# Expert tiles from two lists, the last sequence's routing among the tiles, ten sequences' sums beside the last 39 tiles

## The chip, the core and the metric

The kernel runs on one core of a Trainium2 chip. Times are device microseconds (us) of one execution. The engines are TensorE (PE; its weight loads are PEld), VectorE (DVE), ScalarE (ACT), GpSimd (POOL) and SyncE (SP); SP, ACT and POOL also issue transfers (DMA). Each engine works through its own instructions in order, and waits for the others on semaphores.

## What is computed

16 sequences of 512 tokens with 128 features pass a state-space mixer, then a layer of 8 experts of which each token takes the best 2. Cut to what matters here:

```python
x = layernorm(x + mixer(x))                     # sequence by sequence: conv, scan in chunks of 128, gate
gates = sigmoid(u @ centroids.T)                # 8192 tokens x 8 experts
topk_vals, topk_idx = top_k(gates, 2)           # two experts for each token
h = gelu(einsum('nd,edf->enf', u, W1) + b1)     # 128 -> 512
outs = einsum('enf,efd->end', h, W2) + b2       # 512 -> 128
x = layernorm(x + sum over the two of gate * out)
```

## The kernel before

It has three stages, one after the other.

**Mixer.** A slot for each sequence s (`slots`, `slot_pe`, `slot_dve` and so on). Beside the scan of sequence s, a slot projects sequence s+1 and routes sequence s-1: normalisation, logits, gates, the two picks, ranks within each expert by matmuls against a mask. The rows of sequence s-2 are written by indirect transfers from POOL (`scatter`, eight for each sequence) into `sorted_rows` in DRAM, which holds a region for each expert. `next_row` counts the rows of each expert. A last slot, 16, routes sequence 15 alone.

**Experts.** When all rows are placed, DVE makes a table of 136 tiles of 128 rows (first row and expert of each), and unused rows are filled with padding (`write_pads`). Then, for tile j: SP loads the 128 rows (`xs`, ring of 8); PE transposes them (L631), multiplies by the expert's W1 (`up`, L637) and, after ACT's gelu (L856), by W2 (`down`, L649); DVE copies the transposed rows (L1205), the expert's W1 (L1209) and b2 (L1210) into place, and after `down` adds the bias (L1218) and scales and adds (L1221); POOL writes the result to `moe_rows` by an indirect transfer (L1450). PE's order in an iteration is transpose(j+2), up(j+1), down(j); DVE's is fetch(j+2), weigh(j). Each of them reads the expert number from the table into a register first (`value_load`). The tiles run in loops that the hardware repeats (`Fori`), but for the first 8 and the last 16, which are written out.

**Last stage.** For each sequence n: SP loads two blocks of 256 KB of `moe_rows`, DVE and POOL add them (L1250, L1464), DVE takes mean and variance (L1265, L1273, L1278), POOL the root (L1470), DVE the bias (L1256), ACT normalises (L877) and issues the store. A partition p holds the tokens p, p+128, p+256 and p+384 of a sequence.

## Time and profile before

| | |
|---|---|
| median of 3 runs | 807.89 us (805.18 to 808.49) |
| profiled execution | 798.2 us, span of its instructions 796.3 us |
| busy over the span | PE 673.3, PEld 548.5, DVE 600.1, ACT 473.8, POOL 465.2 us |
| mixer until PE's last mixer matmul | to about 425 us |
| first to last expert tile (start of `down`) | 467.62 to 740.20 us |
| last stage | from there to 796.3 us |

The span runs from the first to the last instruction. Busy time of PE counts pipelined matmuls, so that a full PE shows 99% and not its peak. An engine's idle time is printed in brackets ahead of an instruction, with what ended it. A line number of the profile is that of the kernel before.

### The profile page before, as it was taken

How to read it: one execution, taken by the hardware profiler on the slowest of the kernel's cores; microseconds unless marked ns; L12 is line 12 of the kernel's file. 1: busy time of each engine (PE TensorE's matmuls, PEld its weight loads, DVE VectorE, ACT ScalarE, POOL GpSimd, SP SyncE). 2: the span in 40 equal slices, each digit the busy share in tenths (PEclk: the TensorE clock that was granted, in tenths of full speed). 3: DMA queues.
4: the chain of work that ended last, by engine and by line, in shares of the span. 5: the costliest groups of instructions: out<-in, count | busy, mean ns of one | idle time of the engine just before them, and what ended most of it. 6: DMA issues, size and time to landing. Idle time of an engine off the chain costs nothing.

```text
span 796.3 us, 21108 instructions
## 1 busy us (share of the span) xinstructions
PE 673.3 (85%) x5092; PEld 548.5 (69%) x5093; DVE 600.1 (75%) x2000; ACT 473.8 (60%) x1179; POOL 465.2 (58%) x642
## 2 busy tenths in 40 slices
PE   7969999999999999999984079999999999999200
PEld 6846666666666566666663069999999999999100
DVE  4388989998999999899974446677766667677485
ACT  3747777677677677677661045555555555555165
POOL 4023377777777777777777715555555555555464
PEclk9999999999999999999997579999999999999755
DMA  9160010111110111110100212222222222222496
GB/s 260 32 240 14 16 41 18 41 32 34 42 41 19 38 31 39 42 33 26 38 18 31 73 46 69 64 62 65 65 66 66 61 63 66 66 66 61 132 302 200
DMA packets 74802, 54.09 MB, mean 68 GB/s; under 512 B 9436, under 2 KB 70111, under 8 KB 74481
## 3 DMA queue, kind: packets, MB, share of 16 engines
q1 hardware_dynamic: 56400, 31.90, 15.3%
q0 software_dynamic: 8448, 16.93, 6.4%
q10 hardware_dynamic: 9888, 4.49, 2.0%
q8 instruction: 29, 0.48, 0.3%
q14 instruction: 37, 0.30, 0.1%
HBM read 31.11 MB, written 22.69 MB: 68 GB/s over the span
## 4 chain that ended last, share of the span: by engine, by line
PE 69%; DVE 9%; issue 8%; POOL 5%; ACT 4%; DMA 3%; DVEq 1%; SPq 0%; ACTq 0%; POOLq 0%
PE pl L637 16%; PE p L649 15%; PE pj L402 4%; PE p L589 4%; PE p L597 3%; POOL sorted_rows L1382 3%; PE p L551 2%; PE pj L631 2%; PE p L545 2%; ACT pair L816 2%; PE pj L410 2%; PE p L499 2%; PE p L527 2%; PE p L410 2%; PE pl L446 2%
## 5 line engine op out<-in xcount | busy, mean ns | idle before, releaser
L1450 POOL DMA_INDIRECT moe_rows<-yv,xs x136 | 147.3, 1083 | 139.4 <-DVE yv L1221 122.0
L856 ACT ACTIVATE L<-pl,b_sb 128x128 f32<-128x128 f32 x544 | 154.9, 368 | 118.8 <-PE pl L637 118.8
L637 PE MATMUL pl<-Btok,M 128*128 128x128 f32 x1088 | 151.8, 283 | 0.9 <-DVE M L1209 0.3
L1382 POOL DMA_INDIRECT sorted_rows<-pair,slot x128 | 128.3, 1002 | 35.2 <-issue 33.6
L929 DVE SCALAR_TENSOR_TENSOR acc<-pj,conv_w_sb,acc 128x511 f32<-128x511 f32 (+2 forms) x192 | 142.5, 742 | 4.0 <-ACT acc L734 1.1
L649 PE MATMUL p<-w,L 128*128 x1088 | 143.9, 275 | 1.6 <-ACT L L856 1.6
L637 PEld LDWEIGHTS pl<-Btok,M 128*128 128x128 f32 x1088 | 133.4, 193 | 5.1 <-DVE M L1209 2.7
L649 PEld LDWEIGHTS p<-w,L 128*128 128x128 f32 x1088 | 132.4, 192 | 2.0 <-issue 2.0
L1205 DVE COPY Btok<-pj 128x128 f32<-128x128 f32 x136 | 39.7, 292 | 76.5 <-PE pl L637 66.8
L734 ACT ACTIVATE acc<-pj,conv_b_sb,conv_w_sb 128x512 f32<-128x512 f32 x64 | 49.5, 773 | 33.1 <-PE pj L402 33.1
L402 PE MATMUL pj<-xT,w_xbc 128*128 128x512 f32 x128 | 66.7, 603 | 0.0
L545 PEld LDWEIGHTS p<-M,Xdt 128*64 128x64 f32 x512 | 27.6, 137 | 51.6 <-issue 49.8
L1395 POOL TENSOR_TENSOR Xdd<-Xdt,cur 128x256 f32<-128x256 f32 x48 | 29.5, 615 | 55.9 <-DVE Xdt L1080 47.4
L631 PE MATMUL pj<-ident,xs 128*128 128x128 f32 x136 | 40.1, 295 | 25.8 <-DMA xs<-sorted_rows 24.0
L1209 DVE COPY M<-w 128x512 f32 x136 | 57.4, 422 | 0.4 <-issue 0.4
L1345 POOL TENSOR_TENSOR gt<-yv,sz 128x256 f32<-128x256 f32 x64 | 47.1, 736 | 11.3 <-DVE yv L1106 10.6
L1221 DVE SCALAR_TENSOR_TENSOR yv<-yv,xs 128x128 f32<-128x128 f32 x136 | 47.8, 352 | 4.8
L1218 DVE TENSOR_TENSOR yv<-p,b2e_mem 128x128 f32<-128x128 f32 x136 | 39.6, 291 | 13.7 <-PE p L649 7.5
L545 PE MATMUL p<-M,Xdt 128*64 128x128 f32 x512 | 42.5, 286 | 8.7 <-issue 5.9
L692 ACT ACTIVATE pl<-pl 128x512 f32<-128x512 f32 x64 | 37.5, 586 | 15.7 <-PE pl L428 15.5
L1003 DVE TENSOR_TENSOR M<-pl,Gm 128x512 f32<-128x512 f32 x64 | 43.9, 686 | 2.0 <-ACT pl L692 1.4
L1080 DVE TENSOR_TENSOR Xdt<-p,cur 128x256 f32<-128x256 f32 x64 | 27.0, 422 | 20.5 <-ACT Btok L802 10.4
(203 smaller groups left out, 1328.4 us busy)
## 6 DMA issues: line engine op xcount, KB each, us to landing
xs<-sorted_rows SPq DMA_DIRECT2D x136, 65.0 KB, 1.8
xres<-in_x SPq DMA_DIRECT2D x16, 256.0 KB, 3.0
w<-in_w SPq DMA_DIRECT2D x2, 2048.0 KB, 10.3
acc<-moe_rows SPq DMA_DIRECT2D x16, 256.0 KB, 4.1
xc<-moe_rows SPq DMA_DIRECT2D x16, 256.0 KB, 5.1
out<-sz ACTq DMA_DIRECT2D x16, 256.0 KB, 5.1
moe_rows<-yv,xs POOLq DMA_INDIRECT x136, 2.4
sorted_rows<-pair,slot POOLq DMA_INDIRECT x128, 2.4
```

Source lines behind the costliest of these rows:

```text
L402: pe.matmul(pj[k % 2][:, :], w_xbc[:, k * P:(k + 1) * P], xT[:, q.n, :], start=True, stop=True).then_inc(proj_psum, 1)
L545: mm = pe.matmul(p7[half, (h // 2) * P:(h // 2 + 1) * P], Xdt[c % 2][:, h * HD:(h + 1) * HD], M[c % 2][:, h, :], start=(h < 2), stop=(c == ...
L631: pe.transpose(pj[k % 2][:, 0:P], xs[k][:, 0:P], ident[:, :]).then_inc(sT_psum, 1)
L637: mm = pe.matmul(pl[k % 2][:, f * P:(f + 1) * P], w1e[k % 2][:, f * P:(f + 1) * P], sT[k % 2][:, :], start=True, stop=True)
L649: mm = pe.matmul(o[:, 0:P], hT[k % 2][:, f, :], w2[:, bass.ds(e, 1), f, :].rearrange("p e d -> p (e d)"), start=(f == 0), stop=(f == FB - 1))
L734: act.activation(acc[:, c, :], pj[c % 2][:, :], ACT.Identity, bias=conv_b[:, c:c + 1], scale=conv_w[:, c, TAPS - 1:TAPS]).then_inc(tap0_do ...
L856: act.activation(hT[k % 2][:, f, :], pl[k % 2][:, f * P:(f + 1) * P], ACT.Gelu, bias=b1[:, bass.ds(e * FB + f, 1)]).then_inc(hT_ready, 1)
L929: ins = dve.scalar_tensor_tensor(out=acc[:, k, j:TOKS], in0=pj[k % 2][:, 0:TOKS - j], scalar=conv_w[:, k, TAPS - 1 - j:TAPS - j], in1=acc[ ...
L1209: dve.tensor_copy(w1e[k % 2], w1[:, bass.ds(e, 1), :].rearrange("p e f -> p (e f)")).then_inc(w1e_ready, 1)
L1221: dve.scalar_tensor_tensor(out=ye[k % 4], in0=ye[k % 4], scalar=xs[k][:, P + 1:P + 2], in1=xs[k][:, 0:P], op0=ALU.mult, op1=ALU.add).then_ ...
L1382: pool.indirect_dma_start(out=sorted_rows[:, :], out_offset=bass.IndirectOffsetOnAxis(slot[q.par][:, c, k:k + 1], 0), in_=(rowA, rowB)[k][ ...
L1450: pool.indirect_dma_start(out=moe_rows[:, :], out_offset=bass.IndirectOffsetOnAxis(xs[k][:, P:P + 1].bitcast(I32), 0), in_=ye[k % 4], in_o ...
```

## The change

- **Two lists of tiles.** The first 72 tiles (`FULL`) are whole tiles of the rows of the first 10 sequences (`EARLY`). Their table is worked out on DVE in slot 15 in two parts (`early_table`), with the tile number along the partitions, and goes to DRAM and back by two small transfers to lie in one partition (`table_away`, `table_back`). The other 63 tiles have a second list, made among tiles 4 to 40.
- **Routing among the tiles.** Slot 16 is gone. Tiles start after slot 15, and the routing of sequence 15 and the last steps of 14 are set between tiles 0 to 53 on all engines; POOL's last 16 scatters stand at every third tile. The 8 pad writes all stand on SP ahead of the load of tile 46.
- **Sums beside tiles.** From tile 94 on, one of the first ten sequences' final steps stands in every 4 tiles: DVE's addition at the first, statistics at the second, moments and variance at the third, POOL's root at the fourth, ACT's output 8 tiles later. SP loads its two blocks after the row load of tile 97+4n. Six sequences are left for the last stage.
- **Four consecutive tokens per partition** in the last stage, so that a partition's piece of a block is 2 KB and no longer four pieces of 512 B.
- 135 tiles and not 136, all written out with no hardware loop; the tile buffers lie in `xT` and no longer in the scan's buffers.

```diff
-TILES = 2 * TOKENS // P + E
+TILES = 2 * TOKENS // P + E - 1
+EARLY = 10
+FULL = 72
+COVER = 88
+LATE = TILES - FULL
+SEGS = 2 * E
+FIN_TILES = 4
+FIN_AT = COVER + 6
...
-        sT = Btok
-        w1e = [M[i][:, :, :].rearrange("p h s -> p (h s)") for i in range(2)]
-        hT = L
+        w1e = [xT[:, i, :] for i in range(2)]
+        hT = [xT[:, 2 + i, :].rearrange("p (f s) -> p f s", f=FB) for i in range(2)]
+        sT = [xT[:, 4, i * P:(i + 1) * P] for i in range(2)]
         b2e = [b2e_mem[:, i, :] for i in range(4)]
-        ye = [yv[i // 2][:, i % 2, :] for i in range(4)]
+        ye = [xT[:, 5, i * P:(i + 1) * P] for i in range(4)]
...
-        out_seq = out.rearrange("b (c p) d -> b p c d", p=P)
-        moe_seq = moe_rows.rearrange("(k b c p) d -> b p k c d", k=2, b=SEQS, p=P)
+        out_seq = out.rearrange("b (p c) d -> b p c d", p=P)
+        moe_seq = moe_rows.rearrange("(k b p c) d -> b p k c d", k=2, b=SEQS, p=P)
...
-            for k in range(-1, SEQS + 1):
+            for k in range(-1, SEQS):
...
+            def table_away(k, lo, hi):
+                dq.wait_ge(found_ready, k + 1)
+                dq.dma_start(tile_list[lo:hi, :], found[k][0:hi - lo, :]).then_inc(table_out, 16)
+            def table_back(k, lo, hi):
+                dq.wait_ge(table_out, 16 * (k + 1))
+                dq.dma_start(table[0:1, 2 * lo:2 * hi],
+                             tile_list[lo:hi, :].rearrange("j k -> (j k)").unsqueeze(0)).then_inc(table_in, 16)
+            def load_rows(j):
+                k = j % RING
+                table_known(dq, j)
+                wait(dq, rows_out[k], 16 * (j // RING))
+                at = dq.value_load(table[0:1, 2 * j:2 * j + 1], min_val=0, max_val=SPARE + (E - 2) * P)
                 dq.dma_start(xs[k][:, :], sorted_rows[bass.ds(at, P), :]).then_inc(xs_in[k], 16)
-            for k in range(RING):
-                load_rows(k, k, 0)
-            with dq.Fori(1, TILES // RING) as i:
-                for k in range(RING):
-                    load_rows(RING * i + k, k, i)
-            for k in range(RING):
-                dq.wait_ge(rows_out[k], 16 * TILES // RING)
-            def load_moe(turn, i):
-                n = FIN * turn + i
+            def load_moe(n):
+                i = n % FIN
                 wait(dq, moe_sum, n - FIN + 1)
                 wait(dq, fve_ready, n - FIN + 1)
                 for k in range(2):
                     dq.dma_start(yy[i][:, k], moe_seq[n, :, k]).then_inc(yy_in[i], 16)
-            for i in range(FIN):
-                load_moe(0, i)
-            with dq.Fori(1, SEQS // FIN) as turn:
-                for i in range(FIN):
-                    load_moe(turn, i)
+            table_away(0, 0, FULL)
+            table_back(0, 0, FULL)
+            for i in range(2):
+                for k in range(2):
+                    dq.wait_ge(scattered[i][k], 16 * NC * EARLY // 2)
+            for j in range(TILES):
+                if j == 46:
+                    write_pads(dq, range(E))
+                if j == 56:
+                    table_away(1, FULL, TILES)
+                if j == 60:
+                    table_back(1, FULL, TILES)
+                if j == FULL:
+                    dq.wait_ge(pads_in, 16 * E)
+                    dq.wait_ge(spare_in, 16 * E)
+                    for i in range(2):
+                        for k in range(2):
+                            dq.wait_ge(scattered[i][k], 16 * NC * SEQS // 2)
+                load_rows(j)
+                if j == COVER + RING:
+                    for k in range(RING):
+                        dq.wait_ge(rows_out[k], 16 * COVER // RING)
+                if j > COVER + RING and (j - COVER - RING - 1) % FIN_TILES == 0:
+                    load_moe((j - COVER - RING - 1) // FIN_TILES)
+            for k in range(RING):
+                dq.wait_ge(rows_out[k], 16 * ((TILES - 1 - k) // RING + 1))
+            for n in range(EARLY, SEQS):
...
+            def transpose_rows(j):
+                pe.wait_ge(xs_in[j % RING], 16 * (j // RING + 1))
+                wait(pe, fetched, j - 1)
+                pe.transpose(pj[j % 2][:, 0:P], xs[j % RING][:, 0:P], ident[:, :]).then_inc(sT_psum, 1)
+            def up(j):
+                pe.wait_ge(w1e_ready, j + 1)
+                wait(pe, hT_ready, FB * (j - 1))
+                for f in range(FB):
+                    mm = pe.matmul(pl[j % 2][:, f * P:(f + 1) * P], w1e[j % 2][:, f * P:(f + 1) * P],
+                                   sT[j % 2], start=True, stop=True)
+                mm.then_inc(h_psum, 1)
...
+                if not project:
+                    transpose_rows(0)
+                    transpose_rows(1)
...
+                if not project:
+                    up(0)
...
+            for j in range(TILES):
+                if j == 10:
+                    turn_rows(last)
+                if j == 14:
+                    logits(last)
+                if j == 24:
+                    ranks(last)
+                if j + 2 < TILES:
+                    transpose_rows(j + 2)
+                if j + 1 < TILES:
+                    up(j + 1)
+                down(j)
...
+            for j in range(TILES):
+                if 4 <= j < 4 + NC:
+                    normalise(last, j - 4)
+                if j == 12:
+                    keep_turned(last)
+                if j == 13:
+                    second_rows(last)
+                if j == 16:
+                    exp_logits(last)
+                n, step = divmod(j - FIN_AT - 8, FIN_TILES)
+                if 0 <= n < sent and step < 2:
+                    finish(n, step)
+                if 0 <= n < sent and step == 2:
+                    send(n)
+                gelu(j)
...
+            def early_table(part):
+                full = starts[:, 0, :]
+                if part == 0:
+                    count_tiles(starts[:, 0:2, :])
+                    in_table(dve.tensor_copy(q_tiles[:, 0:E], full))
+                    tiles_ahead(E, E)
+                    return
+                in_table(dve.scalar_tensor_tensor(out=jump[:, 1:E + 1], in0=ends[:, 0:E], scalar=-float(P),
+                                                  in1=seg_row[:, 0:E], op0=ALU.mult, op1=ALU.add))
+                row_steps(E)
+                find_tiles(0, E)
...
+            def fetch(j):
+                e = expert_of(dve, j)
+                wait(dve, h_psum, j - 1)
+                dve.wait_ge(sT_psum, j + 1)
+                dve.tensor_copy(sT[j % 2], pj[j % 2][:, 0:P]).then_inc(fetched, 1)
+                dve.tensor_copy(w1e[j % 2], w1[:, bass.ds(e, 1), :].rearrange("p e f -> p (e f)")).then_inc(w1e_ready, 1)
+                dve.tensor_copy(b2e[j % 4], b2[:, bass.ds(e, 1), :].rearrange("p e d -> p (e d)")).then_inc(b2e_ready, 1)
...
+            for j in range(TILES):
+                if j == 0:
+                    statistics(last)
+                if j == 1:
+                    take_ranks(Seq(0, SEQS - 2))
+                if j == 2:
+                    shift_rows(last)
+                if j == 4:
+                    late_starts()
+                if j == 18:
+                    gate_values(last)
+                if j == 19:
+                    gate_tops(last)
+                if j == 20:
+                    gate_places(last)
+                if j == 21:
+                    gate_picks(last)
+                if j == 26:
+                    take_ranks(last)
+                if j == 27:
+                    dve.wait_ge(rank_read, SEQS)
+                    dve.tensor_copy(pad_at[:, :], next_row[:, :]).then_inc(pads_known, 1)
+                if j == 30:
+                    late_counts()
+                if j == 33:
+                    tiles_ahead(SEGS + 1, SEGS)
+                if j == 36:
+                    late_jumps()
+                if j == 38:
+                    row_steps(SEGS + 1)
+                if j == 40:
+                    find_tiles(1, SEGS + 1)
+                n, step = divmod(j - FIN_AT, FIN_TILES)
+                if 0 <= n < EARLY and step == 0:
+                    add_rows(n)
+                if 0 <= n < EARLY and step == 1:
+                    out_statistics(n)
+                    if n > 0:
+                        minus_mean(n - 1)
+                if 0 <= n < EARLY and step == 2:
+                    out_moments(n)
+                    out_variance(n)
+                if j + 2 < TILES:
+                    fetch(j + 2)
+                weigh(j)
...
+            root_rows(Seq(0, SEQS - 1))
+            place_rows(Seq(0, SEQS - 2))
+            for j in range(TILES):
+                for r, first in ((Seq(0, SEQS - 2), 2), (Seq(0, SEQS - 1), 32)):
+                    at, step = divmod(j - first, 3)
+                    if 0 <= at < 2 * NC and step == 0:
+                        scatter(r, at % NC, at // NC)
+                if j == 29:
+                    place_rows(Seq(0, SEQS - 1))
+                n, step = divmod(j - FIN_AT, FIN_TILES)
+                if 0 <= n < EARLY and step == 0:
+                    add_experts(n)
+                if 0 <= n < EARLY and step == 3:
+                    root(n)
+                store(j)
```

`fetch` and `weigh` are DVE's steps of a tile as before, with one more semaphore; `late_starts`, `late_counts`, `late_jumps`, `row_steps`, `tiles_ahead` and `find_tiles` are chains of small DVE operations on 8 to 272 elements, each of which waits for the one before it.

How the order moves, at three places. DVE, one tile before (one of the last 16), from the bias addition on; `TENSOR_LOAD` is the read of the expert number:

```order
L1218 TENSOR_TENSOR yv<-p,b2e_mem 128x128 [waits rows_out0,b2e_ready,ye_psum]
L1221 SCALAR_TENSOR_TENSOR yv<-yv,xs 128x128 [waits biased]
L1200 TENSOR_LOAD table
L1200 ISA x2
L1205 COPY Btok<-pj 128x128 [waits sT_psum,h_psum]
L1209 ISA
L1209 COPY M<-w 128x512
L1210 ISA
L1210 COPY b2e_mem<-b_sb 128x128
```

DVE after, from the bias addition of tile 95 into tile 96, where `BN_AGGR` and L1375 are the moments and the variance of sequence 0 in the last stage:

```order
L1235 TENSOR_TENSOR xT<-p,b2e_mem 128x128 [waits rows_out3,b2e_ready,ye_psum]
L1238 SCALAR_TENSOR_TENSOR xT<-xT,xs 128x128 [waits biased]
L1368 BN_AGGR fmv<-fst 128x2 [waits fin_step,const_ready]
L1368 BN_AGGR fmv<-fst 128x2 x3
L1375 TENSOR_SCALAR fve<-fmv 128x4 [waits fin_step]
L351 TENSOR_LOAD table [waits table_in]
L351 ISA x2
L1225 COPY xT<-pj 128x128 [waits sT_psum,h_psum]
L1226 ISA
L1226 COPY xT<-w 128x512
L1227 ISA
```

The last-stage work stands between the scaling of a tile and the read for the next fetch, so the copies of the next W1 come behind it.

PE at the end of slot 15 before, with `ones,ysq` and `w_out,gt` the last mixer products, `chosen` the ranks and `ident,pair` the first step in routing sequence 15:

```order
L589 MATMUL p<-ones,ysq 128x96 x8
L597 MATMUL p<-w_out,gt 128x128 x8
L613 MATMUL p<-chosen,ones_b 128x32
L614 MATMUL p<-chosen,before_b 128x32
L617 MATMUL p<-chosen,ones_b 128x24
L617 MATMUL p<-chosen,ones_b 128x16
L617 MATMUL p<-chosen,ones_b 128x8
L570 MATMUL p<-ident,pair 128x128 x4
L575 MATMUL p<-w_gate,uT 128x96 x4
L613 MATMUL p<-chosen,ones_b 128x32
```

PE after, at the same place, with L585 the transposes of tile rows and L591 `up`:

```order
L653 MATMUL p<-ident,carried 128x128 x2
L585 MATMUL pj<-ident,xs 128x128 x2
L686 MATMUL p<-ones,ysq 128x96 x8
L694 MATMUL p<-w_out,gt 128x128 x8
L591 MATMUL pl<-xT 128x128 x4
L574 MATMUL p<-chosen,ones_b 128x32
L575 MATMUL p<-chosen,before_b 128x32
L578 MATMUL p<-chosen,ones_b 128x24
L578 MATMUL p<-chosen,ones_b 128x16
L578 MATMUL p<-chosen,ones_b 128x8
L585 MATMUL pj<-ident,xs 128x128
L591 MATMUL pl<-xT 128x128 x4
```

The transposes of tiles 0 and 1 now stand ahead of the last mixer products, `up` of tile 0 ahead of the ranks of 14, and nothing of sequence 15's routing is left there.

SP before, where the loads of rows enter the loop:

```order
L368 DMA xs<-sorted_rows 128x130
L372 UNCONDITIONAL_BRANCH
L372 ISA
L367 ISA
L367 TENSOR_LOAD table
L367 ISA x2
L368 ISA
L368 DMA xs<-sorted_rows 128x130
```

SP after, from the load of the rows of tile 45 on:

```order
L405 TENSOR_LOAD table
L405 ISA x2
L406 ISA
L406 DMA xs<-sorted_rows 128x130
L357 TENSOR_LOAD pad_at
L357 ISA x2
L358 ISA
L358 DMA sorted_rows<-pad_tile 128x130
```

Such a read of `pad_at` and the pad write behind it come eight times on SP before the rows of tile 46 are loaded.

## Rows read from the trace of the kernel before

**Rows 1.** Windows: stretch, length, PE, PEld, DVE, ACT, POOL busy, granted clock, DMA share, GB/s.

```profile
420.00:430.00 10.00, 4.18 (x37) 3.92 (x37) 5.84 (x37) 0.98 (x3) 8.72 (x12) 0.92 0.11 35
430.00:440.00 10.00, 3.43 (x17) 2.71 (x17) 2.86 (x21) 2.38 (x6) 6.04 (x11) 0.50 0.08 27
500.00:600.00 100.00, 98.64 (x835) 95.38 (x835) 68.75 (x245) 55.86 (x196) 54.83 (x49) 1.00 0.25 64
```

**Rows 2.** Timeline from slot 15 to the first tile: start, duration, instruction, idle before.

```profile
414.70 0.42 DVE L1080 TENSOR_TENSOR Xdt<-p,cur 128x256 f32<-128x256 f32 x1 [2.36 <-ACT Btok L802]
...
423.26 2.05 PE L597 MATMUL p<-w_out,gt 128*128 128x128 f32 x16 [0.37 <-POOL gt L1345]
...
446.27 0.17 DVE L1171 TENSOR_SCALAR tb<-tb 128x8 f32<-128x8 f32 x1
446.48 0.17 DVE L1172 CAST tbi<-tb 128x8 int32<-128x8 f32 x1
...
447.15 4.12 SPq L323 DMA_DIRECT2D sorted_rows<-pad_tile  x4
...
459.64 8.09 SPq L368 DMA_DIRECT2D xs<-sorted_rows  x8
...
461.54 0.45 PE L631 MATMUL pj<-ident,xs 128*128 128x128 f32 x1 [23.24 <-DMA xs<-sorted_rows]
...
465.05 1.28 ACT L856 ACT_TABLE_LOAD   x1 [29.82 <-PE pl L637]
```

**Rows 3.** Timeline: one looped tile's copy, then one written-out tile.

```profile
525.41 0.29 DVE L1205 COPY Btok<-pj 128x128 f32<-128x128 f32 x1 [0.48 <-PE pl L637]
...
718.67 0.35 DVE L1221 SCALAR_TENSOR_TENSOR yv<-yv,xs 128x128 f32<-128x128 f32 x1
...
719.38 0.29 DVE L1205 COPY Btok<-pj 128x128 f32<-128x128 f32 x1 [0.36 <-PE pl L637]
719.46 1.14 ACT L856 ACTIVATE L<-pl,b_sb 128x128 f32<-128x128 f32 x4 [0.77 <-PE pl L637]
719.59 0.42 DVE L1209 COPY M<-w 128x512 f32 x1
...
720.06 0.97 PEld L637 LDWEIGHTS pl<-Btok,M 128*128 128x128 f32 x8
...
720.26 0.29 DVE L1218 TENSOR_TENSOR yv<-p,b2e_mem 128x128 f32<-128x128 f32 x1
```

**Rows 4.** Timeline of PE: `down` of tiles 0, 8, 120, 134 and 135.

```profile
467.62 1.15 PE L649 MATMUL p<-w,L 128*128 x8 [1.10 <-ACT L L856]
...
483.68 1.06 PE L649 MATMUL p<-w,L 128*128 x8
...
711.49 0.72 PE L649 MATMUL p<-w,L 128*128 x5
...
738.62 1.06 PE L649 MATMUL p<-w,L 128*128 x8
740.20 1.15 PE L649 MATMUL p<-w,L 128*128 x8 [0.52 <-ACT L L856]
```

**Rows 5.** Timeline of the last stage: first sequences, and the last addition.

```profile
748.94 0.56 DVE L1250 TENSOR_TENSOR xc<-acc 128x384 f32<-128x384 f32 x1 [6.87 <-DMA acc<-moe_rows]
...
749.91 0.87 DVE L1265 BATCH_NORM_STATS2 fst<-xc 128x6 f32<-128x128 f32 x4 [0.41 <-POOL xc L1464]
750.89 0.38 DVE L1273 BATCH_NORM_AGGREGATE fmv<-fst 128x2 f32<-128x6 f32 x4
...
751.94 0.82 POOL L1464 TENSOR_TENSOR xc<-acc 128x128 f32<-128x128 f32 x1 [2.13 <-DMA acc<-moe_rows]
752.37 0.42 DVE L1278 TENSOR_SCALAR fve<-fmv 128x4 f32<-128x4 f32 x1
...
752.87 1.04 POOL L1470 TENSOR_TENSOR frs<-fve,neg_half 128x4 f32<-128x4 f32 x1
...
786.36 0.52 DVE L1250 TENSOR_TENSOR xc<-xc 128x384 f32<-128x384 f32 x1
```

539 lines of the change are left out of this document (269 added, 270 removed).

## Prediction

> **What bounds the kernel now.** I read the windows by stage first, then the timeline at the two changes of stage, then single tiles. In the expert stage PE is busy 98.64 of 100 us and DVE 68.75 [rows 1], so PE looks like the only limit. The timeline of one tile says more [rows 3]. After the scaling L1221 (start 718.67, 0.35 us) DVE sits idle for 0.36 us and then copies rows and W1; the W1 copy ends at 719.59 + 0.42 = 720.01, and PE's next `up` loads weights at 720.06. The bias addition of the next tile follows at 720.26. So DVE goes round in the same time as PE and has no slack: what stands between L1221 and L1209 delays `up`. The 0.36 us is the read of the expert number: 0.71 us from the start of L1221 to the copy, half of it behind L1221. In a looped tile the idle is 0.48 us [rows 3], for there DVE also has to compute addresses. That shows in the pace: tiles 8 to 120 take 711.49 - 483.68 = 227.81 us, 2.034 us each; the written-out tiles 120 to 134 take 27.13 us, 1.938 us each [rows 4].
>
> Between the stages PE stands still. Its last mixer product of weight starts at 423.26 (2.05 us); the first rows are asked for at 459.64, transposed at 461.54, and `down` of tile 0 starts at 467.62 [rows 2, 4]. From 740.20, the last `down` [rows 4], to the end at 796.3 are 56.1 us in which PE has nothing. There the 16 additions L1250 start from 748.94 to 786.36 [rows 5], 37.42 us over 15 intervals, 2.495 us each.
>
> **The change, part by part.** All times are in the profiled execution (span 796.3, execution 798.2 us).
>
> *Start of the tiles.* The first list costs DVE 7 small chained steps in chunk 0 of slot 15 and 9 in chunk 1. Such steps of 8 elements follow each other at 446.48 - 446.27 = 0.21 us [rows 2]: 1.5 and 1.9 us. The first part has no cover that I see and moves the slot by 1.5 us. The second fits into DVE's idle 2.36 us ahead of 414.70 [rows 2] and ends near 416.1. Two small transfers follow; the nearest row is a row load, 461.54 - 459.64 = 1.9 us [rows 2], so 3.8 us; then a read (0.7) and the load (1.9): rows of tile 0 at 422.5, of tile 1 1.0 us later (8 loads take 8.09 us on SP [rows 2]). PE's transposes of both stand ahead of products that would start about 422.4 now, so PE waits until near 423.9; L597 moves from 423.26 to about 426.3, `up` of tile 0 ends near 429.3. ACT loads its gelu table (1.28 us [rows 2]) and takes 1.14 us [rows 3]: `down` 0 at 432.0. DVE meanwhile does the statistics of sequence 15 (0.87 + 0.38 and gaps [rows 5]) before it fetches tile 2; its W1 is there at 432.5, and with `up` and `down` of 0.97 us each behind it `down` 1 starts at 434.2. Bounds: 430 if the transfers hide wholly, 439 if each takes 2 us more.
>
> *Pace.* All tiles are written out, and DVE's rows of a tile are the same instructions as in the last 16 before, so 133 more tiles at 1.938 us: 257.8 us. At the looped pace it would be 12.8 us more; that is the upper bound.
>
> *Routing and second list among tiles 1 to 53.* An addition of x between L1221 and the read costs x less what the 0.36 us hides; where the read itself waits for the last step, it costs x + 0.35. DVE: 21 chained steps at 0.21 (two of 272 elements at 0.4) and five such reads, 6.6 us; ranks of 14 and 15 and the four pieces of the gates, 3.8 us: 10.4. PE: 4 transposes, 4 logit and 5 rank matmuls, about a tile's worth, 2.1. ACT: the exponential at tile 16 changes the table and back, 2 x 1.28 + 0.2, less its 0.77 idle [rows 3] and the 0.5 before `down` needs it: 1.5; its other pieces of 0.4 to 0.6 us fit the idle. SP: 8 pad writes at 4.12/4 = 1.03 us [rows 2] hold the load of tile 46 for 8.2 us. That load can go when tile 38 is stored, about 7.3 us before PE wants it, and lands in 1.9: 5.5 us are covered, 2.7 stall. POOL's scatters and `place_rows` fit: 54.83 us busy of 100 [rows 1]. Sum 16.7 us; bounds 8 (half of DVE hidden) and 22.
>
> *Sums beside the last tiles.* For each sequence DVE gets an addition 0.56, statistics 0.87 with a bias 0.16, moments 0.38 with a variance 0.16 [rows 5], the two 0.16 as small steps go [rows 2]. By the rule above: 0.35 + 0.56 + 0.03 - 0.71 = 0.23; 0.35 + 1.03 + 0.03 - 0.71 = 0.70; the variance waits for the moments, so 0.41 + 0.05 + 0.35 = 0.81. That is 1.74, and I take 1.9 since POOL and DVE disturb each other (next part): 19 us for ten. Bounds: all 2.13 us less three times 0.36, 1.05 us; and all 2.13 plus a read and gaps, 2.6 us. ACT's halves of 0.83 us fit its 0.77 idle and the 0.5 behind; POOL has half a tile free. Each transfer has about 4.4 us from its issue to DVE's addition.
>
> *POOL beside DVE.* The variance L1278 takes 0.42 us at 752.37 while POOL's addition runs from 751.94 for 0.82 us [rows 5]; a step of that kind takes 0.17 alone [rows 2]. So they do hold each other up by some 0.25 us a time, and the 1.9 above has 0.16 for it. The Trainium skill (SBUF — State Buffer, SBUF: two separate sides) says that the port pair that both share is an exclusive lock for a whole instruction, taken by GpSimd and by VectorE's two-port copies. This trace shows the 0.42 us, no copy beside a root. By that rule ten sums would cost up to POOL's 1.86 us each more, 18.6 us, and not 1.6.
>
> *End.* Ten intervals less in the last stage: 10 x 2.495 = 25.0 us. Two waits for transfers go too, with 2 KB pieces, 0.6 us: bounds 0 and 3. Left: 56.1 - 25.6 = 30.5 us.
>
> **Sum.** 434.2 + 257.8 + 16.7 + 19.0 = 727.7 for the last `down`, plus 30.5: a span of 758.2 against 796.3, 38.1 us less. The execution of 798.2 us would be 760.1. The median of the runs, 807.89, lies 9.7 us above the profiled one; I take the same 38.1 us off it: 769.8, said as **770 us**.
>
> **Rivals.**
> - *More of DVE's work hides* than I count: 1.05 us a sum (-8.5) and half of 10.4 (-5): 756 us. For it: the read may run beside several queued steps. Against: `up` starts right on the heels of the copy [rows 3].
> - *POOL's instructions lock out DVE's copies.* POOL's root of 1.04 and addition of 0.82 us [rows 5] would each stop DVE if it comes to L1209, L1210 or L1221, about half of its time: 10 x 0.93 = 9 us more, 779 us. For it: the 0.42 us. Against: a root is 4 elements and may hold nothing for most of its time. The skill's rule above is this one.
> - *The blocks come late.* DVE waits in order at L1250, ahead of the next fetch. If a pair of blocks takes 6.5 us and not some 4, ten waits of 2 us: 790 us. Against: tile traffic is 64 GB/s [rows 1], and only one pair is under way.
> - *PE's clock falls, slower than before.* It was granted 0.92 with PE busy 4.18 of 10 us, and 0.50 at 3.43 of 10 [rows 1]. If the gaps of up to 0.8 us beside the last 39 tiles lowered it to 1.2 GHz, PE would need 1.94 us more a tile; 20 tiles use up the 38.1 us, all 39 would give 770 + 76 = 846 us. Against: PE stays about 80% busy there, twice what kept 0.92.
> - *Nothing gained*: the written-out code stalls on its own fetches by 0.28 us a tile. The 14 written-out tiles at 1.938 us speak against it.
>
> **Chances.** Forecast 0.55 (760 to 780), more hides 0.15, lock 0.16, late blocks 0.07, slower clock 0.04, nothing 0.03. The range that holds 8 in 10 takes in the second and third and part of the fourth: 755 to 786. A measurement of this kernel can tell about 0.5% from no change. Faster by over 0.5%: 0.93; within it: 0.03; slower: 0.04.
>
> **What would show it.** `down` of tile 1 near 434 with the granted clock 1.00 through 420 to 440; tiles without additions at 1.94 us; a stall of PE near tile 46 with SP's pads ahead of it; groups of four tiles from 94 on at 7.75 + 1.9 = 9.7 us, with the gap ahead of `up` ended by DVE's W1 copy; L1209's copies longer than 0.42 us if the lock is real; no idle of DVE on `moe_rows` blocks in the tiles; 30.5 us from the last `down` to the end. The prediction is wrong if DVE's additions cost nothing, or if the gap before tile 0 stays.

## The result, and the profile after

The changed kernel takes 798.08 us (median of 4 runs, 796.57 to 801.27) beside 806.94 us for the kernel before on the same chip: 0.992 of it, with an interval of 0.989 to 0.994. So it is faster, by 0.8% and not by the forecast 4.7%. The profiled execution took 799.25 us with a span of 797.4 us, 1.1 us more than that of before. The profiled execution of before, 798.2 us, is 8.7 us quicker than the median of its runs; that of after is 1.2 us slower than its own. So the spans below miss the forecast by 39 us, and the medians by 28 (798.08 beside 770).

Set beside the steps of the forecast, the span of 797.4 splits up like this:

| step | forecast | measured | difference |
|---|---|---|---|
| `down` of tile 1 | at 434.2 | at 442.13 | +7.9 |
| tiles 1 to 59 | 129.1 us | 600.55 - 442.13 = 158.4 us | **+29.3** |
| tiles 59 to 94 | 67.8 us | 668.84 - 600.55 = 68.3 us | +0.5 |
| tiles 94 to 134 | 96.5 us | 764.91 - 668.84 = 96.1 us | -0.4 |
| from the last `down` to the end | 30.5 us | 797.4 - 764.91 = 32.5 us | +2.0 |

(129.1 is 58 tiles at 1.938 and the 16.7 us of routing; 96.5 is 40 tiles and the 19 us of sums.) The windows of after, with the columns of [rows 1], show the same:

```profile
430.00:440.00 10.00, 8.31 (x55) 8.11 (x55) 5.74 (x37) 2.42 (x5) 4.61 (x5) 0.74 0.25 62
440.00:460.00 20.00, 14.98 (x115) 14.27 (x116) 10.49 (x43) 9.50 (x33) 10.67 (x18) 0.89 0.14 38
500.00:600.00 100.00, 81.07 (x645) 76.87 (x644) 57.14 (x212) 43.01 (x152) 48.54 (x57) 0.95 0.23 64
600.00:660.00 60.00, 58.92 (x524) 58.44 (x523) 43.05 (x155) 34.68 (x123) 30.22 (x32) 1.00 0.27 71
```

From 500 to 600 PE, full before with 98.64 of 100 us [rows 1], is busy 81.07, and no other engine is fuller than it was. From 600 on it is full again. So something stops the engines again and again in the first 58 tiles.

Beside the last 39 tiles the time in all is as forecast. PE's `down` of tiles 94 to 98:

```profile
668.84 1.06 PE L601 MATMUL p<-w,xT 128*128 x8
672.00 1.06 PE L601 MATMUL p<-w,xT 128*128 x8
674.29 1.06 PE L601 MATMUL p<-w,xT 128*128 x8
676.68 1.06 PE L601 MATMUL p<-w,xT 128*128 x8
678.57 1.06 PE L601 MATMUL p<-w,xT 128*128 x8
```

The four intervals of 3.16, 2.29, 2.39 and 1.89 make 9.73 us; the forecast said 9.7. (The sum agrees, the parts don't; see the section on why the prediction was wrong.)

Which wait is it in tiles 1 to 59? The list of waits from 440 to 760 us (engine, line, what ended the wait: us in all, times, longest) has two entries whose ender the profile can't name, and before has none of this kind:

```profile
DVE xT L1235 <- remote: 21.8, 11, 5.4
ACT xT L919 <- remote: 19.5, 6, 5.6
```

41.3 us together, in part at the same time. L1235 is the bias addition behind `down`, L919 the gelu behind `up`; both wait for PE. One of these places, in the timeline (lines of PEld and of others left out):

```profile
498.03 0.97 POOL L1613 DMA_INDIRECT moe_rows<-xT,xs  x1 [0.71 <-issue]
...
498.55 1.16 PE L591 MATMUL pl<-xT 128*128 128x128 f32 x8
...
499.30 0.96 POOL L1546 DMA_INDIRECT sorted_rows<-pair,slot  x1 [0.30 <-issue]
...
499.55 1.06 PE L601 MATMUL p<-w,xT 128*128 x8
...
500.57 0.98 POOL L1613 DMA_INDIRECT moe_rows<-xT,xs  x1 [0.30 <-issue]
...
502.42 1.14 ACT L919 ACTIVATE xT<-pl,b_sb 128x128 f32<-128x128 f32 x4 [3.46 <-remote]
502.47 0.29 DVE L1235 TENSOR_TENSOR xT<-p,b2e_mem 128x128 f32<-128x128 f32 x1 [0.87 <-remote]
```

`up` (L591) ends at 499.71 by the trace, and ACT's gelu starts 2.71 us later. `down` (L601) ends at 500.61, and DVE's addition starts 1.86 us later. ACT and DVE go on within 0.05 us of each other. Such places are found by what stands ahead of them: POOL issues a routing scatter (L1546) between two stores (L1613), each 1.27 us behind the last, and everything goes on 3.1 us after the scatter's start. 502.42 - 499.30 is 3.12; the places at 476.41, 510.84, 540.67 and 548.30 stand 3.1 to 3.2 us behind scatters at 473.3, 507.7, 537.5 and 545.2. The change sets 16 scatters among tiles 2 to 53, and 29.3 / 16 = 1.8 us. They make 13 such places. The first two, at 449.89 and 455.18, stand in a row of six transfers without a gap and share the longest: `gelu` starts at 455.92 behind an `up` that ended at 451.41. Those at 554.34 and 561.74 have the next store 2.3 and 4.4 us behind them and make none.

I call such a place a hold. Theory H: the holds are the missing time, and they come from the scatters. Rivals: P, POOL's time for a scatter makes the stores late; F, the written-out code waits for its own fetches; D, DVE's added work and cross waits.

### The profile page after: what moved, and what is told of

Its sections match the earlier page's. It is cut to its first block, busy times and chain, and to the rows that moved or that the text cites. A ratio compares the mean times of both kernels' runs of the same rounds, so it can differ in the third digit from the quotient of the medians.

```text
span 797.4 us, 20105 instructions
## 1 busy us (share of the span) xinstructions
PE 678.0 (85%) x5075; PEld 549.4 (69%) x5075; DVE 591.9 (74%) x2009; ACT 474.0 (59%) x1176; POOL 455.3 (57%) x648
## 4 chain that ended last, share of the span: by engine, by line
PE 60%; issue 12%; DVE 12%; ACT 4%; POOL 3%; DMA 3%; another core or an unknown queue 2%; SPq 2%; DVEq 2%; ACTq 0%; POOLq 0%
PE pl L591 9%; PE p L601 9%; PE pj L455 5%; PE p L686 4%; PE p L653 4%; PE p L694 3%; PE p L647 3%; PE p L629 3%; PE p L552 2%; PE p L566 2%; PE p L463 2%; PE p L662 2%; POOL moe_rows L1613 2%; PE pl L499 2%
## 5 line engine op out<-in xcount | busy, mean ns | idle before, releaser
L919 ACT ACTIVATE xT<-pl,b_sb 128x128 f32<-128x128 f32 x540 | 153.5, 368 | 153.6 <-PE pl L591 114.5
L1613 POOL DMA_INDIRECT moe_rows<-xT,xs x135 | 135.0, 1000 | 148.5 <-DVE xT L1238 92.5
L591 PE MATMUL pl<-xT 128*128 128x128 f32 x1080 | 151.6, 284 | 27.5 <-DVE xT L1226 24.0
L601 PE MATMUL p<-w,xT 128*128 x1080 | 148.3, 282 | 18.1 <-ACT xT L919 17.9
L591 PEld LDWEIGHTS pl<-xT 128*128 128x128 f32 x1080 | 134.1, 195 | 38.8 <-DVE xT L1226 31.7
L601 PEld LDWEIGHTS p<-w,xT 128*128 128x128 f32 x1080 | 135.4, 197 | 20.4 <-issue 20.1
L1546 POOL DMA_INDIRECT sorted_rows<-pair,slot x128 | 127.7, 998 | 32.6 <-issue 32.6
L1235 DVE TENSOR_TENSOR xT<-p,b2e_mem 128x128 f32<-128x128 f32 x135 | 39.0, 289 | 53.2 <-PE p L601 26.1
L1225 DVE COPY xT<-pj 128x128 f32<-128x128 f32 x135 | 39.3, 291 | 52.4 <-PE pl L591 23.5
L1226 DVE COPY xT<-w 128x512 f32 x135 | 57.2, 424 | 0.2 <-issue 0.2
L1238 DVE SCALAR_TENSOR_TENSOR xT<-xT,xs 128x128 f32<-128x128 f32 x135 | 48.4, 359 | 4.8
L585 PE MATMUL pj<-ident,xs 128*128 128x128 f32 x135 | 37.7, 279 | 6.4 <-DMA xs<-sorted_rows 6.4
```

Source lines behind the costliest of these rows:

```text
L591: mm = pe.matmul(pl[j % 2][:, f * P:(f + 1) * P], w1e[j % 2][:, f * P:(f + 1) * P], sT[j % 2], start=True, stop=True)
L601: mm = pe.matmul(o[:, 0:P], hT[j % 2][:, f, :], w2[:, bass.ds(e, 1), f, :].rearrange("p e d -> p (e d)"), start=(f == 0), stop=(f == FB - 1))
L919: act.activation(hT[j % 2][:, f, :], pl[j % 2][:, f * P:(f + 1) * P], ACT.Gelu, bias=b1[:, bass.ds(e * FB + f, 1)]).then_inc(hT_ready, 1)
L1226: dve.tensor_copy(w1e[j % 2], w1[:, bass.ds(e, 1), :].rearrange("p e f -> p (e f)")).then_inc(w1e_ready, 1)
L1238: dve.scalar_tensor_tensor(out=ye[j % 4], in0=ye[j % 4], scalar=xs[k][:, P + 1:P + 2], in1=xs[k][:, 0:P], op0=ALU.mult, op1=ALU.add).then_ ...
L1546: pool.indirect_dma_start(out=sorted_rows[:, :], out_offset=bass.IndirectOffsetOnAxis(slot[q.par][:, c, k:k + 1], 0), in_=(rowA, rowB)[k][ ...
```

## The experiments

Ratios are to the kernel before on the same chip, whose median was 803.34, 802.35, 797.12, 797.45, 796.26 and 802.04 us in the six sets. The changed kernel was not run again in these sets; its 0.992 is 796.7 us on the first chip and 790.5 on the third, each to within some 2 us.

**Scatters replaced by POOL's work.**

```diff
-                        scatter(r, at % NC, at // NC)
+                        pool.tensor_tensor(idle_out[:, 8 * (first == 32) + at, :], neg_half[:, :], neg_half[:, :], ALU.pow)
```

The rows of the last two sequences are then never placed; to keep the tiles whole, 32 more pad blocks are written at the start, and two sums read other rows.

> The changed kernel with its 16 scatters among the tiles (sequences 14 and 15) replaced by 16 POOL powers of 128x4 (about 1.04 us each, as the scatter's 0.97 us of POOL), so the rows of these two sequences are never placed and their sums read sequence 13; loads, stores and products keep their number. Theory H (a scatter between two stores holds back what PE signals, and everything goes on 3.1 us after the scatter's start): the stalls of tiles 5 to 57 go, tiles 1 to 59 take about 129 us instead of 158, the whole about 798 - 29 = 769 us. Rival P (it is POOL's time, which makes the stores late): no change, 798. Rival F (the written-out code waits for its own fetches) and rival D (VectorE's added work and cross waits): no change, 795 to 799.

Measured: 767.77 us, 0.958 (0.954 to 0.962), 28.9 us less than the changed kernel there. H holds; P, F and D fall as causes of these 29 us, for POOL has the same time, the code is as long, and DVE's work is all there. `down` of tiles 1 and 59:

```profile
438.96 1.06 PE L606 MATMUL p<-w,xT 128*128 x8
...
568.67 1.06 PE L606 MATMUL p<-w,xT 128*128 x8
```

That is 129.7 us beside the forecast 129.1, so the term for routing and second list was right in sum. Not all of the 29 us is time in holds. The windows of tiles 1 to 59, the changed kernel's first:

```profile
442.00:600.00 158.00, 126.01 (x1002) 119.69 (x1001) 87.73 (x338) 70.90 (x241) 77.39 (x92) 0.95 0.22 59
439.00:569.00 130.00, 116.89 (x1008) 112.72 (x1007) 86.98 (x338) 71.32 (x242) 80.02 (x92) 1.00 0.24 64
```

The granted clock is 0.95 beside 1.00, and PE is busy 9 us longer for about the same products. So up to 9 of the 29 us are products at the slower clock, behind the longer holds; they are counted in the 1.8 us a scatter.

**Each scatter twice**, the second into a tensor that nothing reads:

```diff
                         scatter(r, at % NC, at // NC)
+                        scatter_again(r, at % NC, at // NC)
```

> The changed kernel with each of the 16 scatters among the tiles issued twice, the second time into a tensor that nothing reads. H: each hold lasts one indirect transfer (1.27 us) longer, 16 x 1.3 = 21 us more, about 819 us; with the second not adding to the hold, 798. Rival P: at most 16 x 1.3 less what the 0.9 us gaps of POOL take back, 800 to 810. F and D: no change.

Measured: 814.58 us, 1.016 (1.012 to 1.020), 17.9 us more than the changed kernel, 1.1 us for each second scatter. H said 21.

**The same in the looped kernel before**, behind every fourth store, with 128 rows, with 16 rows, and as a transfer without offsets:

```diff
                     oob_is_err=False).then_inc(rows_out[k], 16)
+                if k % 4 == 3:
+                    pool.indirect_dma_start(
+                        out=rows_again[:, :],
+                        out_offset=bass.IndirectOffsetOnAxis(slot[1][:, k // 4, 0:1], 0),
+                        in_=rowA[1][:, k // 4, :], in_offset=None).then_inc(again, 16)
```

> The kernel before, tile loops still in hardware loops, with one more scatter of the last sequence's rows (into a tensor that nothing reads) behind every fourth store: 34 scatters between stores. H: 34 stalls of some 1.8 us, about 807 + 61 = 868 us. If the hold needs something of the changed kernel, or P: POOL has 34 x 1.3 = 44 us more in 136 gaps of 0.9 us = 122 us, so no change, 807 to 812. F, D: 807.

> The kernel before with an extra scatter behind every fourth store as in the last extra-scatter run, but of 16 rows instead of 128. If the hold goes with the work of the transfer (descriptors and packets): nearly none, 803 to 812 us. If it goes with the instruction (0.97 us of POOL and a second one close behind): the full 1.8 us each, about 864 us.

> The kernel before with, behind every fourth store, a direct transfer of the same 128 rows from POOL's queue (no offsets) in place of the extra scatter. If any transfer that POOL issues between two stores holds what PE signals: about 864 us. If it has to be an indirect one: 803 to 806 us.

Measured: 864.28 us, 1.076 (1.072 to 1.080) with 128 rows; 864.77 us, 1.076 (1.073 to 1.079) with 16; 801.95 us, 0.999 (0.998 to 1.001) without offsets. 60.9 us for 34 scatters are 1.79 us each. So the hold isn't a matter of the changed kernel's code, nor of rows and packets; it takes the indirect instruction. (The direct transfers stood as close, 0.96 to 1.20 us behind one store and 0.9 to 1.8 ahead of the next, and took 0.59 us of POOL each.) The Trainium skill (DMA: Bandwidth & Descriptors, SWDGE vs HWDGE vs iDMA) says that a core of GpSimd computes and writes the descriptors for direct and indirect transfers alike. That gives no reason why one should hold and the other not; the runs show that they differ. The hold in the looped kernel, with 128 rows:

```profile
548.16 1.20 POOL L1453 DMA_INDIRECT moe_rows<-yv,xs  x1 [0.99 <-issue]
...
549.56 1.06 PE L652 MATMUL p<-w,L 128*128 x8
549.66 0.97 POOL L1458 DMA_INDIRECT rows_again<-pair,slot  x1 [0.30 <-issue]
...
550.93 0.99 POOL L1453 DMA_INDIRECT moe_rows<-yv,xs  x1 [0.30 <-issue]
...
552.58 0.29 DVE L1221 TENSOR_TENSOR yv<-p,b2e_mem 128x128 f32<-128x128 f32 x1 [1.93 <-remote]
```

The extra transfer needn't be a scatter of rows, nor be there at all. In the run with direct transfers one place holds, and there three of the kernel's own stores follow one another, 1.3 us apart:

```profile
661.41 0.99 POOL L1453 DMA_INDIRECT moe_rows<-yv,xs  x1 [0.30 <-issue]
...
662.41 1.06 PE L652 MATMUL p<-w,L 128*128 x8
...
662.71 0.99 POOL L1453 DMA_INDIRECT moe_rows<-yv,xs  x1 [0.31 <-issue]
...
664.00 0.98 POOL L1453 DMA_INDIRECT moe_rows<-yv,xs  x1 [0.30 <-issue]
...
665.74 0.29 DVE L1221 TENSOR_TENSOR yv<-p,b2e_mem 128x128 f32<-128x128 f32 x1 [1.99 <-PE p L652]
```

`down` ends at 663.47 and the addition starts 2.27 us later, 3.03 us behind the store in the middle. The changed kernel has such a place too, far behind its scatters: stores at 653.74 and 655.02, `down` ended at 655.26, the addition at 656.61. So the scatters matter because they bring indirect transfers close together, where stores alone mostly stand 1.9 us apart. But not every close row holds: in the kernel before four stores from 702.70 to 706.57 hold nothing.

**The kernel before with its tile loops written out**, nothing else:

```diff
-            with pe.Fori(0, (TILES // RING - 3) // 2) as i:
+            for i in range(0, (TILES // RING - 3) // 2):
```

> The kernel before with its tile loops written out (constants for the table's places) and nothing else changed. H and D: a tile takes 1.90 instead of 1.94 us, 807 - 4 = 803 us. F: stalls like those of tiles 1 to 59, 0.5 us a tile, up to 807 + 68 = 875 us, or 0.28 us a tile, 840 us.

Measured: 789.12 us, 0.983 (0.979 to 0.987). Writing out is worth more than I had said (4 us), and more than the whole change brings. F falls once more. (This run too has a hold between stores alone, at 693.02, 694.31 and 695.60: the addition starts 2.0 us behind its `down`.)

**More room between the transfers**: a scatter every fourth tile, with small POOL copies ahead of it, behind it and ahead of the stores.

```diff
-                    at, step = divmod(j - first, 3)
+                    at, step = divmod(j - first, 4)
...
+                        apart(6 * j)
                         scatter(r, at % NC, at // NC)
+                        apart(6 * j + 1)
```

> The changed kernel with its 16 scatters every fourth tile instead of every third, and a small POOL copy (128x2) before and behind each and ahead of the stores of tiles 3 to 64, so that an indirect transfer starts about 1.5 us or more after the one before instead of 1.27. If a hold comes from two indirect transfers that start 1.27 us apart and 1.5 is far enough: the stalls go, about 770 us. If it comes from three within two tiles (four times 1.9 us with a scatter among them), whatever the gap: no change, 797 us; if the small copies only make the stores later, up to 810.

Measured: 795.57 us, 0.994 (0.991 to 0.997), where the changed kernel's 0.992 is 795.7 us: no gain. The room grew by less than meant: the scatters started 1.33 to 1.47 us behind one store, and the next store mostly 1.43 to 1.74 us behind them, where 1.5 or more had been the aim. The hold behind the scatter at 498.72 ends 2.94 us later, as before. So this room makes no difference; more wasn't tried.

**A bounds check on stage 1's scatters**:

```diff
-                    in_=(rowA, rowB)[k][q.par][:, c, :], in_offset=None).then_inc(scattered[q.par][k], 16)
+                    in_=(rowA, rowB)[k][q.par][:, c, :], in_offset=None,
+                    bounds_check=SPARE + E * P - 1, oob_is_err=False).then_inc(scattered[q.par][k], 16)
```

> The kernel before with a bounds check on its 128 scatters of stage 1, as the stores have one; they start 1.27 us apart in threes and fours there already. If it is the checked kind of indirect transfer, close behind another, that holds what PE signals: stage 1 gets longer, by up to 14 slots x 4 pairs x 1.8 us = 100 us, and surely by over 20. If the check has no part in it: no change, 803 to 807 us.

Measured: 804.62 us, 1.002 (1.000 to 1.004). Stage 1 still has scatters 1.27 us apart and no holds, with the check as without it, which leaves the question what the tiles have that stage 1 lacks: register loads. (By the answer below no hold can arise in stage 1 at all, so this run doesn't clear the check where tiles run. Every hold seen has a store, which has the check, within 1.5 us; a scatter with it beside tiles wasn't tried.)

**Constants in place of register loads** (so that the products use the wrong expert's weights), on all three engines, then on TensorE alone:

```diff
             table_known(eng, j)
-            return eng.value_load(table[0:1, 2 * j + 1:2 * j + 2], min_val=0, max_val=E - 1)
+            return j % E
```

> The changed kernel with the expert's number of a tile a constant (tile modulo 8) on TensorE, ScalarE and VectorE instead of a register load from the table, so the products use the wrong expert's weights; scatters, stores and row loads are as they were. Stage 1 has scatters 1.27 us apart and no stalls, and it has no register loads. If the holds need register loads that meet indirect transfers: the stalls of tiles 1 to 59 go, 797 - 29 = 768 us. If not: 797, less the little that the loads themselves cost (795 to 797).

> The same with a constant on TensorE alone; ScalarE and VectorE still load theirs. If it is TensorE's own register load that makes what it finishes seen late: 768 us. If it is the other engines' loads or none of them: 797 us.

Measured: 759.16 us, 0.951 (0.949 to 0.954), and 765.00 us, 0.960 (0.958 to 0.961), that is 31.3 and 25.5 us less than the changed kernel. No entry with "remote" is left in either list of waits. It is TensorE's register work that meets the scatters.

**The eight scatters of a sequence in one burst**:

```diff
-                    at, step = divmod(j - first, 3)
-                    if 0 <= at < 2 * NC and step == 0:
-                        scatter(r, at % NC, at // NC)
+                    if j == first:
+                        for at in range(2 * NC):
+                            scatter(r, at % NC, at // NC)
```

> The changed kernel with the eight scatters of each late sequence in one burst (ahead of the stores of tiles 2 and 32) instead of one every third tile. A burst takes POOL 8 x 1.27 = 10.2 us, in which stores wait and four tiles go on (7.6 us). If each scatter costs its 1.8 us wherever it stands: 797, or more. If a hold lasts as long as indirect transfers follow one another, with the burst and some eight stores behind it: 2 x (10 to 15) us, 788 to 798. If a burst costs one hold only: 797 - 29 + 2 x (2.6 + 1.8) = 777 us.

Measured: 779.23 us, 0.978 (0.976 to 0.980), which is 11.3 us less than the changed kernel; one hold for each burst would have given 20 less, and a hold that lasts through the burst and eight stores up to 9 less. By the time it is nearer the second, but the trace shows neither. While the scatters go out, 1.27 us apart and beside tiles with TensorE's register loads, nothing is held:

```profile
525.36 1.07 PE L591 MATMUL pl<-xT 128*128 128x128 f32 x8
...
525.79 0.96 POOL L1546 DMA_INDIRECT sorted_rows<-pair,slot  x1 [0.30 <-issue]
...
526.57 1.14 ACT L919 ACTIVATE xT<-pl,b_sb 128x128 f32<-128x128 f32 x4 [0.77 <-PE pl L591]
527.05 0.95 POOL L1546 DMA_INDIRECT sorted_rows<-pair,slot  x1 [0.31 <-issue]
```

`up` ends at 526.43 and `gelu` starts 0.14 us later. PE's `down` then stands still from 452.12 to 462.81 and from 528.85 to 536.78, and these waits have names:

```profile
452.12 1.06 PE L601 MATMUL p<-w,xT 128*128 x8
...
458.27 0.29 DVE L1235 TENSOR_TENSOR xT<-p,b2e_mem 128x128 f32<-128x128 f32 x1 [8.42 <-DMA moe_rows<-xT,xs]
...
460.83 0.47 PE L585 MATMUL pj<-ident,xs 128*128 128x128 f32 x1 [7.66 <-DMA xs<-sorted_rows]
...
462.81 1.91 PE L601 MATMUL p<-w,xT 128*128 x8
```

DVE waits for a store, since it has only four result buffers and the burst has kept POOL from storing them; PE waits for rows, whose buffers come free by stores too. That is rival P, POOL's time, which is real for eight scatters at once. Tiles 1 to 59 take 143.9 us beside 129.7 without scatters, so late stores cost 14 us and the holds are gone. A scatter between scatters holds nothing; why not, where a scatter between stores and stores alone do, stays open.

**The last stage's four consecutive tokens alone**, on top of the written-out kernel before:

```diff
-        out_seq = out.rearrange("b (c p) d -> b p c d", p=P)
-        moe_seq = moe_rows.rearrange("(k b c p) d -> b p k c d", k=2, b=SEQS, p=P)
+        out_seq = out.rearrange("b (p c) d -> b p c d", p=P)
+        moe_seq = moe_rows.rearrange("(k b p c) d -> b p k c d", k=2, b=SEQS, p=P)
```

> The kernel before with its tile loops written out, as in the run before (0.983 of before), and the last stage with four consecutive tokens per partition, its sums all behind the tiles. The last stage was 56.1 us from the last down product for 16 sequences, the DMA engines' share 0.4 to 0.9. If the 512-byte packets bound it: 16 sums at 1.9 to 2.4 us and 20 us of start and end, 50 to 58 less, so 782 to 789 us. If the transfers were hidden: 789 us.

Measured: 782.18 us, 0.981 (0.980 to 0.983), beside 0.983 (0.979 to 0.987) without it. No difference can be told. In the two profiled executions the time from the last `down` to the end is 53.9 us with it and 55.4 without.

**What of TensorE's register work?** Three kernels with the address a constant (the wrong expert's weights): the load kept with its value unused, the address in a register set from the constant and no load, and both. The edit of the last:

```diff
+            if eng is pe_engine[0]:
+                eng.value_load(table[0:1, 2 * j + 1:2 * j + 2], min_val=0, max_val=E - 1)
+                return eng.snap(eng.to_reg(j % E), min_val=0, max_val=E - 1)
```

> The changed kernel with a constant expert on TensorE, as in the run before with 0.960 of before, but with TensorE's register load of the table left in, its value unused (the products use the wrong expert's weights; the register arithmetic of the down product is gone). If it is the load that meets the indirect transfers: the stalls are back, 0.992 of before. If it is the arithmetic or the addressing by register: 0.960.

> The changed kernel with TensorE's register set from a constant (tile modulo 8, wrong expert) instead of loaded from the table; the register arithmetic and the addressing of the down product by register are all there. With the load left in and the arithmetic gone the stalls were gone (0.960 of before). If the arithmetic and addressing alone meet the indirect transfers: the stalls are back, 0.99 of before. If a stall needs both, the loaded value and its use: 0.960.

> The changed kernel with TensorE's register load left in with its value unused, and the down product addressed by a register set from a constant (tile modulo 8, wrong expert): the same 1216 rows of TensorE's queue as in the changed kernel, but the address doesn't hang on the loaded value. If a stall needs only that TensorE's sequencer does both in a tile (its time, 1.4 us of the tile's 1.9): the stalls are back, 0.99 of before. If it needs the address to be the loaded value, or if the constant pattern of experts takes the stalls away by itself: 0.960.

Measured: load alone 765.58 us, 0.960 (0.959 to 0.962); register alone 765.87 us, 0.961 (0.959 to 0.963); both 801.19 us, 0.999 (0.997 to 1.001). Neither alone makes a hold, and both do, although the address doesn't hang on the load and the experts are the wrong ones. The waits of the kernel with both, from 440 to 760 us, have the two entries again (its lines 925 and 1241 are 919 and 1235 of the changed kernel):

```profile
ACT xT L925 <- remote: 24.9, 7, 6.8
DVE xT L1241 <- remote: 21.5, 11, 5.0
```

**The extra scatters with a constant on TensorE**, in the looped kernel before:

```diff
             def expert_of(j):
-                return pe.value_load(table[0:1, 1, bass.ds(j, 1)], min_val=0, max_val=E - 1)
+                return 3
```

> The kernel before with the extra scatter behind every fourth store (1.076 of before) and a constant expert on TensorE in place of its register load (the products use the wrong expert's weights). If a hold needs TensorE's load and an indirect transfer out of step: the 61 us go, 1.00 of before or, with the loads' own cost gone, a little less. If the load matters only beside the changed kernel's written-out code: 1.07.

Measured: 796.77 us, 1.000 (0.999 to 1.001). All 61 us are gone.

**A whole kernel without TensorE's register work.** ScalarE and VectorE copy the expert's second weights into a ring of three, half each.

```diff
+                act.copy(w2e[j % 3][:, 0:FB // 2, :],
+                         w2[:, bass.ds(e, 1), 0:FB // 2, :].rearrange("p e f d -> p (e f) d")).then_inc(w2a_ready, 1)
...
+                dve.tensor_copy(w2e[j % 3][:, FB // 2:FB, :],
+                                w2[:, bass.ds(e, 1), FB // 2:FB, :].rearrange("p e f d -> p (e f) d")).then_inc(w2b_ready, 1)
...
-                e = expert_of(pe, j)
+                pe.wait_ge(w2a_ready, j + 1)
+                pe.wait_ge(w2b_ready, j + 1)
...
-                    mm = pe.matmul(o[:, 0:P], hT[j % 2][:, f, :], w2[:, bass.ds(e, 1), f, :].rearrange("p e d -> p (e d)"),
+                    mm = pe.matmul(o[:, 0:P], hT[j % 2][:, f, :], w2e[j % 3][:, f, :],
```

> A whole kernel: the changed one, with the chosen expert's second weights copied for each tile, half by ScalarE (128x256, some 0.35 us) and half by VectorE (some 0.23 us), so that TensorE reads fixed places and loads no register. If TensorE's load is the cause: 0.960 of before, less what the copies cost; ScalarE has 0.76 us free in a tile and VectorE about 0.3, so some 0 to 0.1 us a tile, 0.960 to 0.975 of before. If it isn't: 0.99 or more.

Then the same with the eight pad transfers one by one:

```diff
-                if j == 46:
-                    write_pads(dq, range(E))
+                if 46 <= j < 46 + E:
+                    write_pads(dq, range(j - 46, j - 45))
```

> The whole kernel with the copied second weights (0.971 of before) and its eight pad transfers one ahead of each row load of tiles 46 to 53 instead of eight in a row ahead of that of tile 46. In the runs without holds the longest single gap was at tile 44 (4.7 to 9 us, 6.9 in this kernel). If it is the pads in a row on SP's queue: 2 to 5 us less, 0.966 to 0.969 of before. If the pads only move their wait: 0.971.

Measured: 773.93 us, 0.971 (0.970 to 0.973), and 770.70 us, 0.969 (0.966 to 0.972). Both beat the kernel before, the changed kernel, and the written-out one. One tile of the first, with the copies at L920 and L1242 and a scatter between two stores that holds nothing:

```profile
559.14 0.99 POOL L1630 DMA_INDIRECT moe_rows<-xT,xs  x1 [0.98 <-DVE xT L1255]
...
560.34 1.06 PE L605 MATMUL p<-xT 128*128 128x128 f32 x8
560.44 0.96 POOL L1563 DMA_INDIRECT sorted_rows<-pair,slot  x1 [0.30 <-DVE xT L1255]
...
561.12 0.38 DVE L1242 COPY xT<-w 128x256 f32 x1
...
561.54 0.28 DVE L1252 TENSOR_TENSOR xT<-p,b2e_mem 128x128 f32<-128x128 f32 x1
561.65 0.42 ACT L920 COPY xT<-w 128x256 f32 x1
561.71 0.98 POOL L1630 DMA_INDIRECT moe_rows<-xT,xs  x1 [0.30 <-issue]
```

`down` ends at 561.40 and DVE adds the bias at 561.54. The single pads can't be told from the eight in a row by the intervals (0.966 to 0.972 and 0.970 to 0.973). In the traces the pause that the eight make, intervals of 6.20 and 3.62 us ahead of tiles 44 and 45, is gone.

## Why the prediction was wrong

**The step that failed** is the routing's: "POOL's scatters and `place_rows` fit: 54.83 us busy of 100". They do fit POOL's time, as the powers in their place show. What they don't fit is between stores beside TensorE's register work: 16 of them cost 29 us, up to 9 of it through the clock that fell behind the longer holds. I priced the scatters by the time of the engine that issues them; no row of before has one between two stores, so I had no row for what they do to others. Its price had to be bounded from both sides, and I took zero as certain. None of the rivals is this one.

**The start** was late by 7.9 us, of which 3.2 are this execution's: in the kernel without scatters tile 1 stands at 438.96, with the same stage 1. (The first transfer goes out at 419.72, in that kernel at 416.89, and the forecast had it near 416.1.) Two things make the rest. The table's way out and back took longer than two row loads:

```profile
419.72 0.37 SPq L394 DMA_DIRECT2D tile_list<-found  x1
...
422.63 0.24 SPq L398 DMA_DIRECT2D table<-tile_list  x1
...
427.04 8.73 SPq L406 DMA_DIRECT2D xs<-sorted_rows  x8
...
428.89 0.47 PE L585 MATMUL pj<-ident,xs 128*128 128x128 f32 x1 [3.25 <-DMA xs<-sorted_rows]
...
430.58 3.57 PE L686 MATMUL p<-ones,ysq 128*128 128x96 f32 x16
...
433.94 2.61 PE L694 MATMUL p<-w_out,gt 128*128 128x128 f32 x16
```

From the first transfer to the row loads are 7.3 us, where the forecast had two times 1.9 and a read of 0.7. And PE's wait for the rows (3.25 us) came just before its clock fell: the granted clock from 430 to 440 is 0.74, not the forecast 1.00, so part of that stretch ran at 1.2 GHz and not at 2.4. L694 took 2.61 us beside 2.05 for the same product before [rows 2].

**What was right.** The pace of written-out tiles: 1.951 us from tile 59 to 94 beside 1.938 (most intervals are 1.90; the one of 3.22 ahead of tile 89 is the hold between stores). The forecast put 12.8 us on the looped pace, and the kernel before gained 14 by being written out (the 4 us in that run's expectation were a slip of mine). The routing's 16.7 us: 129.7 beside 129.1 once the scatters are gone. The pads: in the kernel without scatters PE waits 2.8 us for rows at tile 44, beside 2.7. The sums: 96.1 beside 96.5. The end: 32.5 beside 30.5.

**Right by luck** in part are the sums. The forecast had 0.23 us for the interval with the addition, 0.70 for the statistics and 0.81 for moments and variance. Above 1.905 us they take 0.44, 1.11 and 0.48 in the mean of the ten. The statistics cost more because DVE waits for POOL's part of the addition, 6.0 us in seven of the ten, which the forecast put at nothing ("POOL has half a tile free"):

```profile
681.19 0.87 DVE L1360 BATCH_NORM_STATS2 fst<-xc 128x6 f32<-128x128 f32 x4 [0.68 <-POOL xc L1622]
```

The moments cost less, and the two errors cancel.

**The rivals.** That POOL's instructions lock out DVE's copies showed little: L1226 took 424 ns in the mean, 0.42 us before [rows 3], but L1227 took 0.48 us at 670.87, beside POOL's addition, where 0.22 is usual, and L1238 up to 0.52 where 0.35 is. Over the ten sums such lengthenings add up to some 2.5 us, near the forecast's 1.6 and far from the rival's 9. Late blocks didn't show either: of all DVE's additions from 668 to 765 us one waited for a block, 0.9 us. The clock fell only where PE had waited, from 440 to 460 to 0.89, and was 1.00 from 600 to 660 and beside the last 39 tiles (668 to 765); it followed PE's waits and didn't make them. "Nothing gained" through the code's fetches is refuted by the written-out kernel before.

The four consecutive tokens, for which I had 0.6 us, show nothing that can be told.

## What to carry to other kernels

Price an instruction that moves to another place also by what its new neighbours do to others, and when no row shows the neighbourhood, try it alone in the old kernel first: one extra transfer behind every fourth store would have told 1.8 us each. Operands of TensorE at fixed places, filled by engines that have time left, can be worth their copies: these cost 9 us here (0.971 beside 0.960) and took away holds worth 25 (0.992 to 0.960). And undo the parts one by one before crediting the whole, for writing out the loops alone gave 1.7%, the whole change 0.8%.

## What the hardware showed

An indirect transfer of POOL (not a direct one, and with 16 rows as much as with 128) that stands close between two stores can make what TensorE finishes seen late by ScalarE and VectorE alike, until 2.9 to 3.2 us after that transfer's start, but only while TensorE's queue has a register load and the arithmetic of an address in each tile. Stores alone do it where they follow one another 1.3 us apart; eight scatters in a row didn't, nor did every close row of stores. A scatter between stores cost 1.8 us in the mean, in a looped and in a written-out kernel. TensorE's load takes 0.30 us in the median, 0.65 at most, in the changed kernel (kind, ns min/median/max, first and last start):

```profile
L351 PEldq TENSOR_LOAD <-table x135: 295/301/646, 436.9 to 763.7; - x135
```

So the load itself isn't what waits for 2 us. Whether the products end late or only their signals, why half of the register work is free and the whole is not, and which close rows hold, stays open; the trace models the ends of matmuls, and neither register work beside the scatters of stage 1 nor scatters with a bounds check beside tiles were tried.
